# Four layers on one core: the quarters of wo, R and x moved in the first stages, a longer lag of the summary, and high halves turned on their own in the last stage

## The reference, cut to what matters

```python
x = x + L0_xattn(_layernorm(x), ctx, wq, wk, wv, wo, wk_ctx, wv_ctx, q_norm_w, k_norm_w)
x = x + L0_ffn(_layernorm(x), w_gate, w_up, w_down)
x = x + L1_xattn(_layernorm(x), ctx, Wq, Wg, bg, Wkv, Wo)
x = x + L1_ffn(_layernorm(x), router_gate, expert_gate_up, expert_down)

# L0_xattn: 16 query heads, 4 key/value heads, head size 128
q, k, v = x @ wq, x @ wk, x @ wv                 # q, k: rms_norm, then rope
k_ctx, v_ctx = rms_norm(ctx @ wk_ctx), ctx @ wv_ctx
scores = q @ [k_ctx, k].T / sqrt(128) + causal   # 1601 + 256 keys
out = (softmax(scores) @ [v_ctx, v]) @ wo

# L0_ffn: each linear is act_quant(fwht(x)) @ ternary(w).T
h = h_bitlinear(silu(h_bitlinear(x, w_gate)) * h_bitlinear(x, w_up), w_down)   # 1024 hidden

# L1_xattn: linear attention, 16 heads of 16; f(x) = x + 1 if x > 0 else exp(x)
q, gate = f(x @ Wq.T), sigmoid(x @ Wg.T + bg)
k, v = split(ctx @ Wkv.T)
summary = einsum('bhsd,bhse->bhde', f(k), v); k_sum = f(k).sum(-2)
out = (q @ summary) / (q @ k_sum + eps) * gate @ Wo.T

# L1_ffn: 8 experts of 128, the best 2 by softmax(x @ router.T), silu(gate) * up, down
```

## Time and profile before

| | |
|---|---|
| profiled execution, its own time | 1268.01 us |
| its span in the trace | 1266.2 us |
| PE busy | 1153.8 us (91%), 11339 matmuls |
| PE weight loads busy | 885.1 us (70%) |
| DVE busy | 1011.2 us (80%) |
| ACT busy | 814.2 us (64%) |
| POOL busy | 823.7 us (65%) |
| chain that ended last, by engine | PE 69%, DVE 13%, ACT 6%, DMA 4%, POOL 3%, SP's queue 2% |

### The profile page before, as it was taken

How to read it: one execution, slowest core, us unless ns; L and a number is a source line. 1 busy time by engine, 2 the same in 40 slices (tenths; PEclk the granted TensorE clock), 3 DMA queues, 4 the chain that set the end, 5 groups by cost and what they waited for, 6 DMA issues and landing times.

```text
span 1266.2 us, 30132 instructions
## 1 busy us (share of the span) xinstructions
PE 1153.8 (91%) x11339; PEld 885.1 (70%) x11339; DVE 1011.2 (80%) x1953; ACT 814.2 (64%) x1897; POOL 823.7 (65%) x1010
## 2 busy tenths in 40 slices
PE   3987798999999999999999999999999987568898
PEld 3876476777777787777777777777777766336556
DVE  6675687888888888888888888888888887996752
ACT  4664576777777777777777777767777644337441
POOL 3984586768768596968768696968778632761132
PEclk9999899999999999999999999999999998789899
DMA  9990468767897788788778887777877999131044
GB/s 266 283 198 1 94 158 162 150 153 160 191 180 140 163 158 168 154 177 188 152 160 147 162 151 173 154 155 160 154 151 156 184 188 248 36 67 34 1 76 92
DMA packets 603889, 188.19 MB, mean 149 GB/s; under 512 B 581312, under 2 KB 596816, under 8 KB 603488
## 3 DMA queue, kind: packets, MB, share of 16 engines
q1 hardware_dynamic: 602720, 182.85, 70.3%
q0 software_dynamic: 1024, 3.42, 1.0%
HBM read 32.72 MB, written 8.26 MB: 32 GB/s over the span
## 4 chain that ended last, share of the span: by engine, by line
PE 69%; DVE 13%; ACT 6%; DMA 4%; POOL 3%; SPq 2%; issue 2%; ACTq 0%; POOLq 0%; DVEq 0%
PE PS L1329 15%; PE PS L1331 14%; PE PS L1330 14%; PE PS L1501 7%; PE PS L1497 6%; PE PS L1498 6%; DVE mx L1889 3%; DMA pT_l<-pl 2%; DVE pl L1909 2%; ACT pr L1675 1%; PE PS L1448 1%; PE PS L1457 1%; DVE hh L1050 1%; DVE wo_l L957 1%; DMA stage<-in_ctxT 1%
## 5 line engine op out<-in xcount | busy, mean ns | idle before, releaser
L1889 DVE TENSOR_REDUCE mx<-PS 128x1 f32<-128x512 f32 (+2 forms) x512 | 296.1, 621 | 109.4 <-PE PS L1331 107.8
L1497 PE MATMUL PS<-v_h,pT_h 128*128 128x129 f16 (+1 forms) x1856 | 225.7, 222 | 3.5 <-DMA pT_h<-ph 2.8
L1498 PE MATMUL PS<-v_l,pT_h 128*128 128x128 f16 (+1 forms) x1856 | 225.6, 221 | 0.0
L2136 POOL CAST ph<-pr_end 128x705 f16<-128x705 f32 (+1 forms) x128 | 107.4, 839 | 172.7 <-ACT pr_end L1675 172.6
L1329 PE MATMUL PS<-kT_h,qT_h 128*128 128x512 f16 (+2 forms) x512 | 182.6, 357 | 17.8 <-ACT pr L1675 16.6
L1497 PEld LDWEIGHTS PS<-v_h,pT_h 128*128 128x128 f16 (+1 forms) x1856 | 182.8, 99 | 7.7 <-DMA pT_h<-ph 4.6
L1675 ACT ACTIVATE pr<-PS,nb 128x1024 f32<-128x1024 f32 x128 | 144.3, 1127 | 65.6 <-DVE nb L1897 65.6
L1498 PEld LDWEIGHTS PS<-v_l,pT_h 128*128 128x128 f16 (+1 forms) x1856 | 182.8, 98 | 2.4
L1330 PE MATMUL PS<-kT_l,qT_h 128*128 128x512 f16 (+2 forms) x512 | 181.7, 355 | 0.0
L1331 PE MATMUL PS<-kT_h,qT_l 128*128 128x512 f16 (+2 forms) x512 | 181.6, 355 | 0.0
L1909 DVE TENSOR_TENSOR pl<-pr,ph 128x1024 f16<-128x1024 f32 x128 | 174.8, 1366 | 0.0
(11 more groups left out here) (291 smaller groups left out, 2878.4 us busy)
## 6 DMA issues: line engine op xcount, KB each, us to landing
stage<-in_ctxT SPq DMA_DIRECT2D x8, 800.5 KB, 8.1
weights_kept<-relay SPq DMA_DIRECT2D x30, 128.0 KB, 2.2
ctx_kept<-ctx SPq DMA_DIRECT2D x4, 800.5 KB, 10.6
ctx<-ctx_kept SPq DMA_DIRECT2D x8, 400.2 KB, 4.2
relay<-in_w_lanes SPq DMA_DIRECT2D x14, 204.9 KB, 3.7
stage<-in_wq SPq DMA_DIRECT2D x4, 512.0 KB, 4.7
relay<-in_wo SPq DMA_DIRECT2D x4, 512.0 KB, 4.3
pT_h<-ph SPq DMA_TRANSPOSE x128, 4.0
```

The source lines that it names most:

```text
L1497: mm(PS[:, OB, 0:DH + 1], pT_h[0:rows, slot, t, :], v_h[0:rows, par, v, :], start=t == 0, stop=False)
L1498: mm(PS[:, OB, 0:DH], pT_h[0:rows, slot, t, :], v_l[0:rows, par, v, :], start=False, stop=False)
L1889: dve.reduce_max(mx[:, c:c + 1], PS[:, c, 0:cols(u % LT, c)], AX_X).then_inc(mx_part, 1)
L2136: pool.tensor_copy(ph[:, slot, HALF:LAST + w], pr_end[:, 0:BANK + w]).then_inc(pool_hi, 1)
```

## The change

Four parts:

- **Group 0.** Quarters 0 and 1 of wo are converted in the preparation (jobs n = 1 and n = 7), quarters 2 and 3 in units 0 and 2. The lane load, lane step, piece load and piece halves of group 0 each stand one unit earlier.
- **R.** DVE makes R of the last context before job n = 1, behind the low part of quarter 0; before, it stood before n = 2.
- **First stages.** SP issues the two halves of context 0 ahead of x, and DVE makes their low parts ahead of x's statistics. x is normalised in steps 2 and 3 and turned from step 5 on. The summary runs 5 steps behind the projection and the ring has 7 buffers.
- **Last stage.** SP issues the transpose of the high rows as soon as ACT has made them, and that of the low rows behind the low part. Each has a semaphore of its own. PE does all matmuls that need the high rows, then waits for the low ones. ACT waits, before it writes a high buffer again, for the transpose of the high rows and for the subtraction that reads it; the low part waits for the transpose of the low rows.

```diff
 def lane_at(g):
-    return 2 if g else 5
+    return 2 if g else 4
 def piece_hi_at(g):
-    return 4 if g else 7
+    return 4 if g else 6
 def piece_lo_at(g):
-    return 5 if g else 7
+    return 5 if g else 6
...
-LN_AT = 4
-L1_LAG = 4
-L1_RING = 6
+NORM_AT, LN_AT = 2, 5
+L1_LAG = 5
+L1_RING = 7
...
-        def rows_turned(net, hf, j):
-            return (turned_hi, turned_lo)[hf][j % 2], 8 * NG * UNITS + 32 * (2 * net + j // 2 + 1)
+        def rows_turned(k, net, hf, j):
+            done = ((turned_hi, turned_lo), (turned_q, rows_in))[k][hf][j % 2]
+            first = (8 * NG * UNITS, (32 * NG, 32 * B)[hf])[k]
+            return done, first + 16 * (2 * net + j // 2 + 1)
...
             def rotate_hidden(hf, j):
-                pe.wait_ge(*rows_turned(0, hf, j))
+                pe.wait_ge(*rows_turned(0, 0, hf, j))
...
-                for k in range(FF // D):
-                    for c in range(DC):
-                        f = k * DC + c
-                        for w, t in enumerate((hT_h[hf], hT_l[hf])):
+                for w, t in enumerate((hT_h[hf], hT_l[hf])):
+                    if w:
+                        pe.wait_ge(*rows_turned(1, 0, hf, j))
+                    for k in range(FF // D):
+                        for c in range(DC):
+                            f = k * DC + c
...
             def down_second(hf, j):
...
                 for f in range(NE):
-                    last = three(o, (hT_h[hf][:, j, f * P:(f + 1) * P], hT_l[hf][:, j, f * P:(f + 1) * P]),
-                                 (ed_h[:, f, :], ed_l[:, f, :]), f == 0, f == NE - 1)
+                    mm(o, hT_h[hf][:, j, f * P:(f + 1) * P], ed_h[:, f, :], start=f == 0, stop=False)
+                    mm(o, hT_h[hf][:, j, f * P:(f + 1) * P], ed_l[:, f, :], start=False, stop=False)
+                pe.wait_ge(*rows_turned(1, 1, hf, j))
+                for f in range(NE):
+                    last = mm(o, hT_l[hf][:, j, f * P:(f + 1) * P], ed_h[:, f, :], start=False, stop=f == NE - 1)
...
                 if net or j >= 2:
-                    act.wait_ge(*rows_turned(net - (j < 2), hf, (j + 2) % 4))
+                    act.wait_ge(*rows_turned(0, net - (j < 2), hf, (j + 2) % 4))
+                    act.wait_ge(tl[f"hl{net - (j < 2)}"], nth(f"hl{net - (j < 2)}", hf, (j + 2) % 4))
...
         def hidden_lo(eng, hf, j, net):
             eng.wait_ge(tl[f"hx{net}"], nth(f"hx{net}", hf, j))
+            if net or j >= 2:
+                eng.wait_ge(*rows_turned(1, net - (j < 2), hf, (j + 2) % 4))
...
-            load(0)
+            for i in range(FIRST):
+                load(i)
             sp.dma_start(xs[:, :].rearrange("p (t d) -> p t d", t=TILES),
                          x.rearrange("(t p) d -> p t d", p=P)).then_inc(in_x, 16)
-            for i in range(1, FIRST + 1):
-                load(i)
+            load(FIRST)
...
-                    if g == 0 and 0 < u < KVH:
-                        wo_load(u)
-                    if u == (0 if g else KVH) and g < NG - 1:
+                    if g == 0 and u == 1:
+                        wo_load(3)
+                    if u == (0 if g else 3) and g < NG - 1:
                         lane_load(g)
...
             wo_load(0)
+            wo_load(1)
             for lt in range(LT):
                 turn_queries(lt, 0)
+            wo_load(2)
...
-                sp.wait_ge(tl[f"hl{net}"], nth(f"hl{net}", hf, j))
-                for t, rows_of in ((hT_h, rows_h), (hT_l, rows_l)):
+                for k, (t, rows_of, made) in enumerate(((hT_h, rows_h, f"hx{net}"), (hT_l, rows_l, f"hl{net}"))):
+                    sp.wait_ge(tl[made], nth(made, hf, j))
                     sp.dma_start_transpose(t[hf][:, j, :].rearrange("p (f n) -> p f n", n=P), rows_of[hf][j % 2])\
-                      .then_inc(rows_turned(net, hf, j)[0], 16)
+                      .then_inc(rows_turned(k, net, hf, j)[0], 16)
...
-                    if first and u < KVH:
-                        wo_hi_part(u)
+                    if first and u in (0, 2):
+                        wo_hi_part(2 + u // 2)
...
                 if n == 1:
                     turned_out(B - 1)
+                    wo_hi_part(0)
+                if n == 7:
+                    wo_hi_part(1)
...
-            set_lo_part(0)
+            for i in range(FIRST):
+                set_lo_part(i)
             dve.wait_ge(in_x, 16)
...
-            for i in range(1, FIRST):
-                set_lo_part(i)
...
-                if n < 2:
-                    x_norm(n)
+                if NORM_AT <= n < NORM_AT + 2:
+                    x_norm(n - NORM_AT)
...
-                    if first and u < KVH:
-                        wo_lo_part(u)
+                    if first and u in (0, 2):
+                        wo_lo_part(2 + u // 2)
...
             for n, (kind, i) in enumerate(PREP_JOBS):
-                if n == 2:
+                if n == 1:
+                    wo_lo_part(0)
                     l1_end(B - 1)
+                if n == 7:
+                    wo_lo_part(1)
```

More of the change, by code:

```diff
@@ L753, in rotate_hidden @@
                     pe.wait_ge(tl["ro"], nth("ro", hf, j - 2))
-                for k in range(FF // D):
-                    for c in range(DC):
-                        f = k * DC + c
-                        for w, t in enumerate((hT_h[hf], hT_l[hf])):
+                for w, t in enumerate((hT_h[hf], hT_l[hf])):
[4 more added lines that the diff above has]
+                            f = k * DC + c
                             last = mm(PS[:, bank(hf, 2 * (j % 2) + k // 2), (k % 2) * D:(k % 2 + 1) * D],
-                                      t[:, j, f * P:(f + 1) * P], H0[:, c, :], start=c + w == 0, stop=c + w == DC)
+                                      t[:, j, f * P:(f + 1) * P], H0[:, c, :], start=w + k % 2 + c == 0, stop=w + k % 2 + c == 3)
                 last.then_inc(tl["fw"], 1)
@@ L845, in down_second @@
             def down_second(hf, j):
-                pe.wait_ge(*rows_turned(1, hf, j))
+                pe.wait_ge(*rows_turned(0, 1, hf, j))
                 if j < 2:
```

## The result

The changed kernel takes 1260.99 us, the median of 15 runs (1255.71 to 1263.92), and the kernel before 1269.95 in the same comparison (15 runs). The ratio is 0.9927, with a 95% interval of 0.9914 to 0.9941: faster by 0.6 to 0.9%. In a later comparison with other runs it was 0.9904 (0.9887 to 0.9922). The forecast was 1258.2, or 0.991 of the median then known, in a range from 1252.5 to 1265.5.

What follows compares the result with a forecast made beforehand. PE was taken as full in the steady attention groups, with gains only in four places where it is not: -1.6 - 1.6 - 6.5 - 1.1 = -10.8, so 1268.0 - 10.8 + 1.0 = 1258.2 us, range 1252.5 to 1265.5.

Steps and rivals of the forecast that it cites:

- First stages, -1.6: Up to 104 us: x behind the context wins 2.0 us, near the DMA share's 1.65 us hole; longer lag costs 0.4.
- rival B: First stages: the earlier transposes only queue behind the loads, the stage gives +0.4, total 1260.2 us; chance 0.12.
- R, -2.2: Preparation: with R made first, PE goes on at 111.4 us, not 113.56, and all 2.2 us arrive.
- Quarter 1, +0.6: Preparation: quarter 1's low part stands before piece 6's on DVE, so norm 5 starts 0.6 us later.
- rival C: Preparation: quarter 1's low part holds POOL's scale until its end, costing 0.9 us more, total 1259.1; chance 0.08.
- Group 0, -6.5: Three PE stalls and the low clock behind two go, 7.7 us, less 0.7 for kq2 and 0.5 for missing slack.
- stalls 2 and 3: Group 0: PE stalls of 1.11 us (kq2's low part) and 2.06 us (SP held by piece 0's low part), both to go.
- The first stall: Group 0: PE's 1.27 us stall at 180.95, ACT holding exp 5 behind quarter 3's copy; to go.
- Last stage, -1.1: First network: earlier high transposes shorten DVE's 3.26 us wait for PE's rotation by 1.1 us; second network 0.
- A: Group 0: stalls move, one of 2 us with low clock costs about 3.7, gain only 2.5, total 1262.2; chance 0.20.
- D: Preparation to unit 6: DVE is the bound and starves PE in units 4 to 6, total 1272.1 us, slower; chance 0.07.
- E: PE loses no time in units 4 to 6 and the first network's clock stays up: 1254 us; chance 0.05.

Runs made afterwards that it cites:

- late_turn: late_w with the transposes of context 0 issued ahead of the last context load, which is converted in step 5, not 1: 1251.49 us, ratio 0.986.
- u_lag4: The changed kernel with the summary 4 steps behind the projection and a ring of 6 again, x still behind the context: 1259.54 us, ratio 0.9932.
- after: First trace of the changed kernel; the profiled run took 1261.59 us.
- u_tail: The changed kernel with the last stage as before: 1258.66 us, ratio 0.993.
- u_first: The changed kernel with all first stages as before (x first, lag 4, ring 6): 1258.76 us, ratio 0.9927.
- u_lanes: The changed kernel with lane and piece jobs of group 0 in units 4 to 7 again, quarters of wo still moved: 1262.63 us, ratio 0.9953.
- u_lanes2: The same kernel as u_lanes, run and traced once more: 1263.22 us.
- late_ln: late_w with x normalised in steps 3 and 4 and turned from step 6 on: 1257.73 us, ratio 0.991.
- after2: The changed kernel unaltered, timed and traced again in a later comparison: 1257.03 us, ratio 0.9904.
- late_w: The changed kernel with the wsf loads of contexts 1 and 2 converted in steps 5 and 6, not 3 and 5: 1250.90 us, ratio 0.9862.
- late_w_old: The same line as late_w, in the kernel with the old first stages (x first, lag 4, ring 6): 1254.09 us, ratio 0.9888.
- before2: The kernel before the change, run and traced once more: 1269.58 us.
- u_R: The changed kernel with R made before job 2 again, quarters of wo still in the preparation: 1262.22 us, ratio 0.9948.

## Why the prediction was right or wrong, step by step

**First stages, -1.6: wrong in both halves of the step, nothing in the sum.** Six traces with the new first stages begin the preparation at 102.55 to 107.40, on average 105.3; three with the old ones at 104.79 to 106.39, on average 105.5. The step "what can be won is the hole in the DMA share" failed: asked for 2.4 us earlier, the last transpose landed at 27.4 for 27.8, so 0.4 us came where 2.0 was taken, and one of the forecast's own signs of being wrong was all but met. The turned rows were first used at 28.7, not near 26, and ACT's copy of wsf came at 74.84, not near 72.3. The transposes did queue behind the loads (rival B), as late_turn showed by taking one load away; and the forecast held only POOL's power against the later x, not DVE's norm and PE's turn, which now end PE's wait and stand ahead of the first summary. The longer lag cost the step of exp and relu that was counted (2.09 us for 1.05). Whether it gives anything back isn't shown: the wait for turned rows of 1.90 us before was gone after, but with the lag of 4 it was under 0.4 in u_lag4 as well. That traces of the same first stages can lie 1.6 to 4.9 us apart there was not in the forecast at all. The rows give two sources. From after to u_tail (107.40 and 102.55), 2.8 us are the length of PE's second wait for the summary (4.64 and 1.87), behind a wait of ACT for wsf's DMA of 7.16 and 4.38 us; why that DMA lands at different times stays open. Another 1.7 is a fall of the clock behind that wait, in one and not in the other.

**R, -2.2: right.** "To R" went from 8.77 to 6.59 or 6.60 in every trace that had it. Undone it was 9.91, so R's own place is worth 3.3, of which quarter 0 takes back 1.14. The 2.2 was worked out with the quarter in.

**Quarter 1, +0.6: right, with a small part of rival C on top.** POOL's scale took 1.56 us beside the low part, for 0.70 alone, so rival C's mechanism was there. Its price was not: the chain paid 0.86 in all, where 0.6 was taken and the rival had 0.9 on top of it. DVE was busy until 126.92 by itself, behind the low part and that of piece 6, and the norm started at 127.18; so 0.60 is DVE's order and 0.26 the hold. The slowing agrees with what the Trainium skill says (GPSIMD Engine Reference, Specifications): an instruction of DVE with two SBUF inputs contends with GpSimd. "Prep." as a whole moved by -0.5 to +0.9 in ten of the eleven traces with R early, and by +2.0 in u_first, which isn't explained. In u_tail, u_lanes, u_lanes2 and late_ln the clock fell around the wait for R, and it was 27.6 to 27.7; in after, after2, late_w and late_w_old it did not, and it was 26.7 to 26.9.

**Group 0, -6.5: right, somewhat small.** 119.67 and 120.31 against 111.7 to 112.8 in nine of the ten traces with the new order (114.0 in u_first): about -7.6, nearly the "all gone" of 7.7. The new stall of 0.7 on kq2's low part did not show; 0.64 on POOL stood near. u_lanes2 gives stalls 2 and 3 their price, 4.3 of it. The first stall was read wrongly in one respect: ACT was only one of two engines that were late there. In the kernel before, PE had already stood 0.50 us at 179.27 for POOL's rope of the keys, 1.7 us ahead of its wait for ACT; in before2, u_lanes, u_lag4, u_first and late_turn that rope is what PE waited for, 1.74 to 4.96 us. Taking ACT's copy away didn't remove that risk, and what makes the rope late in some traces stays open.

**Last stage, -1.1: right in place, short in size.** DVE's wait shrank by 1.10 (3.26 to 2.16), as worked out. Half a microsecond more came behind it, up to the maximum that the forecast held to be DVE's own pace (25.13 to 24.69 us from one maximum to the next). In all -1.6 in the first pair of traces. The traces of u_lanes, u_lanes2 and u_lag4 gained only 0.7 to 1.0. In u_R, u_first, late_w_old and late_ln it was 1.2 to 1.7 more than in the changed kernel: 0.5 to 0.75 of it in DVE's wait (1.41 to 1.68 us), 0.6 behind the last maximum of the 1024 values. What makes these four differ isn't explained.

**The sum.** In the two traces of the changed kernel, against the two of the kernel before, the columns are +0.6 - 2.2 - 0.3 - 7.8 + 1.2 - 1.6 = -10.1 on the mean. With means over all traces that have the edit in question it is -0.2 - 2.2 + 0.3 - 7.6 + 0.5 - 1.9 = -11.1. The forecast had -10.8, and the two comparisons give -9.3 and -12.2 by their ratios. The agreement is in part luck, of errors that cancel: 1.4 too much in the first stages, 1.9 too little in group 0 and at the end. Of the rivals, A and D did not occur; B did in the first stages, C with a third of its price, and of E the part on group 0 came near.

## What to carry to other kernels

Ask of an in-order engine what it stands for, and what of another's is queued behind it: a copy that waits for a late DMA held the summary that PE needed, and converting the loads one or two steps later (one line) was worth about 6 us (1250.90 for 1257.03), more per line than anything in the change. When two engines are late for PE at nearly the same place, removing the work of the one that the profile names leaves the other. And before a difference of 2 us between two traces is explained, trace one of the kernels twice.

## What was not expected of the hardware

In these traces POOL (GpSimd) is slowed beside a long DVE instruction by more than the 0.3 us seen before, and DVE's instruction beside a long one of POOL too. At the start of the changed kernel, POOL's low half takes 2.64 us beside DVE's low part of the context, and 1.15 later without it; DVE's f_s takes 1.65 us for 0.69:

```profile
16.64 0.69 DVE L1834 SCALAR_TENSOR_TENSOR f_s<-ex_s,re_s 128x512 f32<-128x512 f32 x1 [1.01 <-ACT re_s L1618]
18.07 1.83 DVE L1802 SCALAR_TENSOR_TENSOR ctx<-stage,ctx 128x1601 f16<-128x1601 f32 x1 [0.74 <-ACT ctx L1591]
18.27 2.64 POOL L2103 TENSOR_TENSOR f_l<-f_s,f_h 128x512 f16<-128x512 f32 x1
19.81 1.65 DVE L1834 SCALAR_TENSOR_TENSOR f_s<-ex_s,re_s 128x512 f32<-128x512 f32 x1
...
26.25 1.15 POOL L2103 TENSOR_TENSOR f_l<-f_s,f_h 128x512 f16<-128x512 f32 x1
```

The fall of PE's clock behind a wait is not decided by the wait's length alone. Waits of 2.14 and 3.80 us were followed by a fall in the first stages, waits of 1.87, 2.82 and 3.57 were not. PE's wait for R was 1.65 us in eleven traces, and the clock fell with it in five of them and not in six. At waits of 5.94 and 7.67 us twice the usual 1.7 us was lost; but there the clock was down some 2 us before the wait ended, while PE stood, so not all of that was time lost.
